# First attention stage: where a projection stands in odd slots, and in what order it takes its PSUM bank

## The reference

```
x = x + attn_a(layernorm(x))        # per sample; 16 heads of width 64
  Q, K, V = X @ Wq, X @ Wk, X @ Wv
  A = softmax(Q K^T / 8, over keys) V
  attn_a = X + gelu(A) @ Wpost
x = x + ffn(layernorm(x))
x = x + attn_b(layernorm(x))        # 16 heads of width 16
x = x + ffn(layernorm(x))
```

## Time and profile before

| | us |
|---|---|
| median of 3 runs | 3819.68 |
| the three runs | 3817.45, 3819.68, 3819.93 |
| the profiled execution | 3818.72 |
| its span in the trace | 3816.9 |

### The profile page before, as it was taken

One profiled execution on the slowest core, in us unless ns is written; L12 is line 12 of the kernel. 1 busy time (PEld: TensorE's weight loads), 2 busy tenths in 40 slices (PEclk: granted clock), 3 DMA queues, 4 the chain that ended last, 5 costly groups with the idle time before them and its releaser, 6 DMA issues.

```text
span 3816.9 us, 64440 instructions
## 1 busy us (share of the span) xinstructions
PE 3635.9 (95%) x23810; PEld 2439.4 (64%) x23810; DVE 2564.6 (67%) x4263; ACT 2384.8 (62%) x4629; POOL 1929.5 (51%) x1370
## 2 busy tenths in 40 slices
PE   8999999999999999999999978999999999999987
PEld 6777777777777777777777654555555555555534
DVE  6766667667666666666667656777677767776662
ACT  5665656565565665656665546767677767677654
POOL 4555555556555555555555534555555444555412
PEclk9999999999999999999999988999999999999988
DMA  2000000000000000000000022222222222222220
GB/s 78 7 12 1 12 12 12 1 12 12 1 12 12 9 4 12 12 1 12 12 1 15 24 58 52 58 58 63 58 58 58 58 58 58 58 58 58 53 47 18
DMA packets 102329, 116.28 MB, mean 30 GB/s; under 512 B 23556, under 2 KB 75268, under 8 KB 102020
## 3 DMA queue, kind: packets, MB, share of 16 engines
q1 hardware_dynamic: 102020, 112.17, 11.9%
HBM read 34.48 MB, written 27.26 MB: 16 GB/s over the span
## 4 chain that ended last, share of the span: by engine, by line
PE 77%; DVE 10%; ACT 6%; issue 4%; POOL 2%; DMA 0%; SPq 0%; DVEq 0%; POOLq 0%; ACTq 0%
PE ps_o L673 12%; PE ps_s L642 10%; PE ps_t L655 8%; PE ps_t L226 8%; PE ps_o L749 5%; PE ps_m L655 4%; PE ps_t L233 4%; PE ps_s L722 4%; DVE max_b L1158 4%; PE ps_m L226 3%; PE ps_t L708 3%; PE ps_t L784 3%; POOL h_lo L567 2%; PE ps_m L233 2%; ACT et L865 2%
## 5 line engine op out<-in xcount | busy, mean ns | idle before, releaser
L532 POOL TENSOR_TENSOR e_a<-e_a,recip 128x1024 f32<-128x1024 f32 x512 | 969.5, 1894 | 949.0 <-DVE recip L1025 948.7
L823 ACT ACTIVATE e_a<-ps_s,neg_max 128x512 f32<-128x512 f32 x1024 | 694.2, 684 | 544.8 <-DVE neg_max L1018 544.4
L1158 DVE TENSOR_REDUCE max_b<-ps_s 128x2 f32<-128x1024 f32 x512 | 624.7, 1220 | 300.9 <-PE ps_s L722 299.5
L865 ACT ACTIVATE et<-ps_s 128x1024 f32<-128x1024 f32 x512 | 526.9, 1029 | 323.7 <-PE ps_s L736 322.1
L1018 DVE TENSOR_REDUCE neg_max<-ps_s 128x2 f32<-128x1024 f32 x512 | 622.3, 1216 | 67.8 <-PE ps_s L642 67.8
L673 PE MATMUL ps_o<-et_a,v_a 128*64 128x256 f32 x4096 | 501.4, 387 | 9.3 <-DVE heads_a L1061 4.8
L642 PE MATMUL ps_s<-raw_a 64*128 64x512 f32 x3072 | 426.1, 409 | 5.4 <-ACT e_a L823 5.3
L567 POOL TENSOR_TENSOR h_lo<-h,h_hi 128x512 fp32r<-128x512 f32 x248 | 317.0, 1287 | 199.2 <-ACT h_hi L917 195.9
L673 PEld LDWEIGHTS ps_o<-et_a,v_a 128*64 128x64 f32 x4096 | 280.0, 137 | 192.7 <-issue 79.4
L655 PE MATMUL ps_t<-ident,e_a 128*128 128x128 f32 x2664 | 394.3, 280 | 0.0
L1032 DVE COPY et_a<-ps_t 128x512 f32<-128x512 f32 x367 | 251.4, 687 | 210.0 <-PE ps_t L655 205.7
(11 more groups left out here) (194 smaller groups left out, 7220.1 us busy)
## 6 DMA issues: line engine op xcount, KB each, us to landing
q_stack<-roped_q SPq DMA_DIRECT2D x256, 96.0 KB
k_stack<-roped_k SPq DMA_DIRECT2D x256, 96.0 KB
x_a<-X SPq DMA_DIRECT2D x16, 512.0 KB, 3.5
X<-x_a SPq DMA_DIRECT2D x16, 512.0 KB, 2.9
x_ahead<-X SPq DMA_DIRECT2D x16, 512.0 KB, 3.8
X<-x_ahead SPq DMA_DIRECT2D x16, 512.0 KB, 2.9
x_before<-X SPq DMA_DIRECT2D x16, 512.0 KB, 3.9
OUT<-x_before SPq DMA_DIRECT2D x16, 512.0 KB, 5.1
```

Source lines behind the costliest of these rows:

```text
L532: nc.gpsimd.tensor_tensor(e_a[:, u % 5, :, :], e_a[:, u % 5, :, :], factor, ALU.mult).then_inc(e_normed, 1)
L823: ins = nc.scalar.activation(e_a[:, u % 5, h, :], ps_s[:, 2 * (u % 2) + h, :], ACT.Exp, bias=neg_max[:, u % 5, h:h + 1], accum_out=sums[:, ...
L865: nc.scalar.activation(et[:, v % 5, :, :], ps_s[:, 2:4, :], ACT.Exp)\
L1158: nc.vector.reduce_max(max_b[:, u // 4 % 2, :, u % 4], ps_s[:, score_bank(u):score_bank(u) + 2, :], AX.X, negate=True).then_inc(max_done, 1)
```

## The change

Two places. In the numbering of fills, an odd slot's first product comes ahead of the two fills of its transposes. In PE's program, an odd slot runs its first product first, then the values, then the transposes, and then what is left of the products (the second x in slot 23). Even slots keep their order. The programs of the other engines are written as before: they wait for the same fills, whose numbers and banks have moved.

```diff
--- before.py
+++ after.py
@@ -336,10 +336,9 @@
 
         steps_of, fill_of, fills = {}, {}, 0
         for slot in range(FIRST_A, LAST + SHIFT):
-            if 0 <= slot < UNITS_ALL:
-                fill_of["turn", 0, slot], fill_of["turn", 1, slot] = fills, fills + 1
-                fills += 2
-            for todo in todo_of.get(slot, []):
+            turns = [("turn", part, slot) for part in range(2)] if 0 <= slot < UNITS_ALL else []
+            others = todo_of.get(slot, [])
+            for todo in (others[:1] + turns + others[1:] if slot % 2 else turns + others):
                 fill_of[todo] = fills
                 fills += 1
             for step in (2 * (slot - SHIFT), 2 * (slot - SHIFT) + 1):
@@ -794,13 +793,16 @@
                     if slot < LAST_A:
                         if slot % 2 == 0 and 0 <= slot + LEAD < UNITS_ALL:
                             a_scores(slot + LEAD)
-                        if slot % 2 == 1 and 3 <= slot < UNITS_ALL:
-                            a_values((slot - 3) // 2)
+                        if slot % 2 == 1:
+                            for todo in todo_of.get(slot, [])[:1]:
+                                a_product(todo)
+                            if 3 <= slot < UNITS_ALL:
+                                a_values((slot - 3) // 2)
                         if slot == UNITS_ALL:
                             a_values(UNITS_ALL // 2 - 1)
                         if 0 <= slot < UNITS_ALL:
                             a_transposes(slot)
-                        for todo in todo_of.get(slot, []):
+                        for todo in todo_of.get(slot, [])[slot % 2:]:
                             a_product(todo)
                     u = slot - SHIFT
                     if 0 <= u < UNITS_ALL:
```

## The result

| | before | after |
|---|---|---|
| median (4 runs each), us | 3819.51 | 3922.73 |
| lowest to highest | 3817.45 to 3819.93 | 3921.84 to 3924.55 |
| profiled execution | 3818.72 | 3924.55 |
| its span | 3816.9 | 3922.7 |

The kernel became slower: the ratio is 1.0275, with a 95% interval of 1.0262 to 1.0287. The prediction was 3914 us, in a range of 3880 to 3940.

What follows compares the result with a forecast made beforehand. PE alone was taken to set the first stage's time, busy 1856.67 of 1870 us. Terms -2 + 41 + 44 + 12 = +95 us on the profiled 3818.72 gave 3913.7, predicted as 3914 us, range 3880 to 3940.

Steps and rivals of the forecast that it cites:

- PE's list: PE's instruction order over 256 pairs of slots: savings and costs of new neighbours cancel; -2 us, bounds -5 and +5.
- Plain waits: Even slots' transposes wait 0.37 us for the odd slot's "qk" bank to be emptied, 111 times: 41 us, bounds 28 to 56.
- Slots 21 to 24: Late DVE and a second x sharing the first's bank add 2.9 us, 15 times: 44 us, from 30 to 58.
- The clock: Idle PE ahead of slot 23's second x lowers the clock in half of 15 samples: 12 us, bounds 0 and 26.
- The bank in time (1): ACT and DVE empty the odd product within the scores' 1.59 us: 3811 us, faster; 3 in 100.
- Only slot 23 pays (2): Plain waits are hidden and only the second x waits: 3873 us; 5 in 100.
- Cheaper transposes (3): Transposes ahead of scores cost no more than ahead of a product, 0.18 us less in 130 pairs: 3891 us; 5 in 100.
- Slot 23 worse (4): Clock falls every time (+14) or late DVE adds 1 us at slots 6 and 22 (+32): 3928 to 3946; 12 in 100.

Runs made afterwards that it cites:

- single-step kernel: The changed kernel, but only the "v" and "post" products of odd slots moved ahead and numbered first; "qk" and x as before: 3813.79 against 3817.54 us, 0.9989.
- slot 23 alone: The kernel before with only slot 23 changed: first x ahead of the values and numbered first, second x behind the transposes: 3875.81 against 3818.52 us, 1.0151.
- with it left: The changed kernel with slot 23 in the order and numbering of before: 3880.79 us, ratio 1.0165.
- ACT first: The changed kernel, but in odd slots ACT makes the high part of the slot's first product ahead of its copy of the transposes: 3878.35 us, 1.0157.
- both first: The changed kernel, slot 23 as before, ACT's high part and DVE's low part of odd slots' first products ahead of their transpose copies: 3884.37 us, 1.0175.
- DVE copies both: The changed kernel, but in slots 1, 9, 13, 17, 25 and 29 DVE copies both banks of the transposes: 3911.26 against 3817.54 us, 1.0247.

## Why the prediction was right, and where its terms were off

The direction and the mechanism held, and the profiled execution grew by 105.8 us where the sum had 95. (The sum's 3913.7 and the 1 us to the median make 3914.7, not 3914; nothing hangs on it.) Term by term:

- **PE's list, -2.** The pairs of slots 8, 16 and 28 are 0.03 to 0.04 us shorter (8.31 to 8.27 or 8.28), that of 12 by 0.01, and those of 4 and 20 are 0.02 longer: -1.3 in sum over those of the table. The neighbours seen above cost what the earlier trace rows said. Right.
- **Plain waits, +41, measured 44.8.** This is two errors that nearly cancel. The chain of copy, high and low part ends at +1.91 for a forecast of +1.90. But I took PE's start at 0.06 us behind a low part, from the x of the earlier trace rows, and here it is 0.15 behind (1063.26 + 0.69 to 1064.10). So a wait is 0.47 us, not 0.37, and 111 of them are 52 us. The term that was mis-sized is the release. Against that stands something I did not see: the values of slots 3 and 19 were late before, by some 0.17 us, and the moved post fills that. It gives back 5.4 us. The single-step kernel shows it alone. The rest, -2 us, is a sum of small things: transposes behind a wait take 0.82 us instead of 0.85 (-3.3), the neighbours save some 0.02 us in these pairs too (-2), and two of the 111 waits were longer, 2.3 and 1.8 us (+3).
- **Slots 21 to 24, +44, measured 48.7.** The working had the last transpose of slot 23 at +8.62, the second x at +10.82 and the scores at +11.41. The trace has +8.50 for the group (8.29 forecast), +11.06 and +11.64. The casts are what moved it: 2.01 us from 1117.87 to 1119.88 where the earlier trace rows had 1.71, because POOL's subtraction, which they end 0.29 us behind, ends later against them now. The runs with slot 23 alone (1.97 of 3.14 us) and with it left (1.18) split it as the prediction did, into the x that waits for its neighbour and a DVE that is late. The second part is read from the trace: no run changed slot 21 alone, or took DVE's heads and normalisation out of the low part's way.
- **The clock, +12, measured 13.6.** Half of the samples was a guess between 0 and 15, and nine fell. That it came out so well is luck: the same idle 1.90 us gave nine falls here, most of 1.5 us, and with slot 23 alone nine of 2.85 us in a row and two shorter ones. With ACT first the x wait only 1.37 us and falls came all the same, in 11 of 15 samples, 13.7 us in the pairs of slot 24; with both first PE idles for 1.54 and 1.31 us, and none came. The idle times in front of an x have transposes on both sides, so PE had done nothing but transposes and waiting since the values; whether that counts with the idle time, no run tests. In the earlier trace rows a product ended ahead of the idle time and scores came behind it, and the clock fell too. What decides in which sample it falls stays open.
- **Rivals.** None of them came. The bank in time (1) would have needed ACT's order changed, as the ACT-first kernel shows. Only slot 23 pays (2): the runs have both. Cheaper transposes (3): they took 1.03. Slot 23 worse (4): the clock fell in nine samples, not in all, and the casts grew by 0.3 us, not by 1.

My expectations were poorer than the prediction. Three kernels that were to remove waits (ACT first, both first, DVE copies both) came out 30 to 73 us above. Each time the edit took away or shortened the wait that I had worked out, and a second chain through the same engine, at slots 6 and 22, was left or made longer. The sum had been made over plain slots, and the slots with gelus, casts and normalisation were taken as equal to them.

The reason for the plain waits is so shown from both sides, and slot 23's part by the run that has it alone and the run that leaves it. Moving the product costs nothing where its bank is emptied in one step, or where ACT's and DVE's lists are turned along and the slot has no other work. It costs 0.45 to 0.47 us where ACT's copy still stands ahead of its high part.

## What to carry to other kernels

When one engine's order is changed, write the order of every engine that frees its buffers beside it: the product of slot 9, which had run up to the scores, ended 2.9 us ahead of them (1059.13 to 1062.04) and freed its bank 0.48 us later (at +1.91 for +1.43), since the engine that empties it kept its list. And price the slots with extra work on their own. With PE busy for 1856.67 of 1870 us there was a gain of 0.1% to be had, a wait of half a microsecond in a fifth of the slots (94 of 512) cost 1.2%, and with slots 5 and 21 to 24 the loss was 2.7%.

## What the runs showed of the hardware

- **VectorE's fp32 to fp32r casts wait for the subtraction on POOL that they meet.** Two casts of 128x512 take 0.75 us alone, 1.79 and 2.09 with POOL's two subtractions (fp32 to fp32r, 128x512, 2.53 and 2.71 us) begun 1.4 and 0.9 us ahead of them, and 2.66 to 2.70 where they begin 0.3 us behind the subtractions' start. In the traces of before, of the changed kernel and of both lists turned, each of the 157 casts that begin while a subtraction runs ends 0.28 to 0.35 us behind the end of that one, also where POOL has begun the next (1116.96 to 1119.67 for the pair above, the casts from 1117.87 to 1119.96). Cut to 16 columns, the subtractions left them at 0.75. In the same traces the maximum (1.20) and the copies out of PSUM (0.68) keep their times while POOL scales exponentials (1.89) beside them.
- **The clock after one idle stretch.** Idle time of 1.90 us on PE, with transposes on both sides, brought the granted clock from 1.00 to 0.50 (1.2 GHz) in 9 of 15 samples, eight times for some 3.4 us and once for 6.8. In the kernel with slot 23 alone the same idle time did so in 11 of 15, nine times for 6.8 us.
- **A release isn't one number.** From the end of DVE's low part to the waiting PE's start it is 0.14 to 0.15 us where PE comes from the scores (1115.62 to 1115.77), and 0.06 where it comes from transposes (1121.75 to 1121.81, 1124.31 to 1124.37). With both lists turned the values, which come behind a product, start 0.14 behind DVE's copy (1097.78 to 1097.92). In the cases of 0.14 the tile's shape changes with the waiting piece (`64*128` to `128*128`, `128*128` to `128*64`), in those of 0.06 it doesn't; whether that is the reason, no run tests.
